# The router's last three pieces, its weights, rank products, list entries and scatters some slots later in the step

## The chip, the core and the metric

One Trainium2 chip, one core. The metric is the device time of one execution of the whole program in microseconds (us). TensorE is PE in the profile (PEld is its weight load), VectorE is DVE, ScalarE is ACT, GpSimd is POOL, SyncE is SP.

## What is computed

A vision-transformer layer on 16 images of 512 tokens with 256 features, plus one class token per image (513 rows). The parts of the reference that matter here:

```python
h = _L0_tok_ref(0, x, W0, W1, Wo)          # relu(x W0) * (x W1), then Wo; per token
h = concatenate([cls_tok, h], axis=1)
h = h + _L0_attn_ref(_layernorm(h), ...)   # quantised projections, 16 heads of 16
h = h + _L0_ffn_ref(_layernorm(h), ...)    # a router picks 2 of 8 experts for each token
# in _L0_ffn_ref:
router_probs = softmax(x_flat @ gate_w)
top_k_probs, top_k_idx = top_k(router_probs, 2)
top_k_probs = top_k_probs / sum(top_k_probs)
```

The kernel doesn't compute all experts for all tokens. It sorts the tokens by expert: for each token it finds the two best experts, the two weights, and a place in each of those experts' lists. Those list entries are written to memory by indirect DMAs (the scatters), and a second phase gathers the listed rows tile by tile.

## The kernel before

The program has a setup, a phase of steps that does everything up to the lists (some 1,680 us), and the expert phase. The change lies in the steps.

**Steps.** One step works on five images at once, each at another stage; in `body(T, P, C, W, X)` image T is in its token layer, P is normalised and projected, C has its attention scores computed, W finishes its attention, and X gets its second residual, its layer norm and its router. In step i, C is image i, T is i+2 and X is i-2. Steps -2 to 2 and 13 to 17 are written out; steps 3 to 12 are five laps of a hardware loop of two steps each, so that every engine jumps back after steps 4, 6, 8 and 10. Steps below are named by the image of C.

**Slots.** A step has 64 slots, `at` = 0 to 63 (group g = at // 16 of four heads, u = at % 16). In every slot PE multiplies one 128x512 block of scores (L493) and one of transposed scores (L502). DVE takes the row maxima of the first (`head_max`, L1147, a head maximum below) and ACT the exponential of the second (L823). PE has two banks for scores: its block of a slot waits for the head maximum of two slots before. In every fourth slot PE multiplies the exponentials by the values (`pv`, L511). Everything else is put into slots by hand: each engine's body asks `if X.ok and at == 47`. Each engine runs its own list in order, and semaphores join them.

**The router of X.** In slot 33 PE makes the logits. DVE's `router` has four pieces, in the slots of the table `ROUTER_AT`: piece 0 finds the largest logit, piece 1 (L1241 to L1243) its place and the one-hot `oh`, piece 2 (L1232 to L1239) masks it and finds the second one, piece 3 (L1241 to L1246) makes the second one-hot and `picked`, the sum of both. ACT makes one small exponential of the difference (L917), and DVE's `weights` (L1255 to L1257) the two weights. PE's `ranks` (L790 to L794) multiplies `picked` by a triangle of ones, which counts how many tokens before this one chose the same expert. DVE's `payload` (L1264 to L1272, then L1432) makes the places and the list entries. Then POOL issues the eight scatters of the image (L974), one for each slot in `SCATTER_AT`; the first waits for `payload`.

**What else is near it.** On DVE: L1436 (`pvd`, slot 36), L1298 (`hid`, 38), L1183 and L1184 (`den`, 39), L1193 and L1194 (`o_sb`, `pr`, 40), two statistics L1442 (slots 43, 44), L1461 and L1462 (45), L1447 and L1449 (46), L1155 and L1157 (end of 47), L1163 to L1456 (48), L1171 to L1472 (49), L1475 to L1478 (52), L1482 and L1484 (53). On PE: the transposes of the maxima (L647, slot 41) wait for `o_sb`; L725 (41, 42), `pv` (43, 47, 51), L750 (44), the token layer's output L562 (46, 49, 53, 57), L759 and L760 (51). On POOL: L1021 and L1025 (slot 35), L991 and L995 (41, after `pr`), L1029 (42, right behind them), which work on whole 128x1024 tiles; then nothing until the scatters; among these W's L1033 (slot 53, after the scatter of this slot), L991 and L995 again (57), and behind the last of them L1040 to L1048 (slot 60), which make the quantised `qi2` and `qic`. PE transposes these in slot 1 of the next step (L588), so L588 waits for L1048:

```python
if X.ok and at == 1:
    wait(pe, s("pool_qi2"), 2, X, 2)
```

Of the kernel before, what the change touches and what calls it, by code (L numbers as in the profile page):

```python
# [40 lines left out]
HIDDEN_AT = (14, 19, 22, 38)  # L41
OUT_AT = (46, 49, 53, 57)
STATS_AT = (53, 54, 60, 61)
ROUTER_AT = (34, 35, 37, 41)
SCATTER_AT = (52, 53, 54, 55, 56, 57, 58, 59)


C_ID, C_TRI = 0, 128
# [49 lines left out]
def fresh(eng, at, *batches):  # L98

    if batches[0].n is None or isinstance(batches[0].n, int):  # L100
        return batches
    n = batches[0].n
    copy = eng.alloc_register(f"lap_{batches[0].k}_{at}")
    eng.reg_mov(copy, n)
    n = eng.snap(copy, min_val=n.min_val, max_val=n.max_val)
    return [At(b.k, n, b.ok) for b in batches]


def wait(eng, sem, per, b, n):

    value = b.v * per + n
    if not isinstance(value, int) or value > 0:
        eng.wait_ge(sem, value)
# [31 lines left out]
def token_phase(nc, outer, images, x_t, cls, w0_t, w1_t, wo_t, attn_w_t, gate_w, consts, out,  # L145
# [12 lines left out]
    def s(name):  # L158

        if name not in sems:  # L160
            sems[name] = nc.alloc_semaphore(f"{name}_{stage}")
        return sems[name]
# [302 lines left out]
    def tensor_program(pe, stage):  # L465
# [49 lines left out]
        def body(T, P, C, W, X):  # L515
            for g in range(NG):
                for u in range(UNITS):
                    if u % 4 == 0:
                        T, P, C, W, X = fresh(pe, UNITS * g + u, T, P, C, W, X)
                        st, tg, mt = in_slot(g, P, C, W)  # L520
                    at = UNITS * g + u
# [193 lines left out]
                    if P.ok and at in (41, 42):  # L715
# [7 lines left out]
                        for t in (2 * k, 2 * k + 1):  # L723
# [1 line left out]
                                last = mm((d0, d1)[k][:, D * (t % 2):D * (t % 2 + 1)], xq[:, c, blk(t)],  # L725
                                          wq_int[:, 2, c, :], start=(c == 0), stop=(c == DC - 1))
                            last.then_inc(s("pe_v"), 1)
                    if X.ok and at == 47:
                        ranks(X, TB, 128, "", [("dve_oc", 1, W, 1)] if W.ok else [("dve_lg", 1, X, 1)])
                    if W.ok and at == 35:  # L730

# [52 lines left out]
        def ranks(b, nt, np_, x, free):  # L784

            wait(pe, s("dve_picked" + x), 1, b, 1)
            for name, per, at_, n in free:
                wait(pe, s(name), per, at_, n)
            a = picked[0:np_, :, :].rearrange("p t e -> p (t e)")
            mm(d2[0:np_, 0:nt * E], tri_bf[0:np_, 0:np_], a[:, 0:nt * E], start=True, stop=(nt == 1))  # L790
            for t in range(1, nt):
                mm(d2[0:np_, t * E:nt * E], ones_bf[0:np_, 0:np_], a[:, 0:(nt - t) * E], start=False, stop=(t == nt - 1))
            for t in range(nt):
                last = mm(d2[:, TB * E:(TB + 1) * E], ones_bf[0:np_, :], a[:, t * E:(t + 1) * E],  # L794
                          start=(t == 0), stop=(t == nt - 1))
            last.then_inc(s("pe_rk" + x), 1)

        if stage == STEPS:
            steps(pe, body)
# [11 lines left out]
    def scalar_program(act, stage):  # L811
# [13 lines left out]
        def body(T, P, C, W, X):  # L825
            for g in range(NG):
                for u in range(UNITS):
                    if u % 4 == 0:
                        T, P, C, W, X = fresh(act, UNITS * g + u, T, P, C, W, X)
                        st, tg, mt = in_slot(g, P, C, W)  # L830
                    at = UNITS * g + u
# [80 lines left out]
                    if P.ok and at == 40:  # L912
                        wait(act, s("pool_rk"), 1, P, 1)
                        f(parts["km"][:, :, :], rest[:, :, :], ACT.Copy).then_inc(s("act_km"), 1)
                    if X.ok and at == 39:
                        wait(act, s("dve_e"), 1, X, 1)
                        f(e21e[:, :], e21[:, :], ACT.Exp).then_inc(s("act_e"), 1)  # L917
                    if P.ok and at in (42, 43, 44, 45):
# [18 lines left out]
        if stage == STEPS:  # L937
            steps(act, body)
# [12 lines left out]
    def gpsimd_program(pool, stage):  # L951
# [16 lines left out]
        def scatter(b, nt, np_, x, pieces):  # L968

            if 0 in pieces:  # L970
                hold(pool, s("dve_pay" + x), 1, b, 1)
            for piece in pieces:
                k, t = divmod(piece, nt)
                g_.indirect_dma_start(out=list_dram, out_offset=bass.IndirectOffsetOnAxis(  # L974
                    ap=slot_i[0:np_, k, t:t + 1], axis=0), in_=pay[0:np_, k, t, :], in_offset=None) \
                    .then_inc(s("scattered"), 16)

        def body(T, P, C, W, X):
            for g in range(NG):
                for u in range(UNITS):  # L980
# [4 lines left out]
                    if u == 9 and tg[0].ok:  # L985
# [9 lines left out]
                        g_.tensor_tensor(o, o, cadd[:, :, :, :], ALU.add).then_inc(s("pool_add"), 1)  # L995
                    if X.ok and at in SCATTER_AT:
                        scatter(X, TB, 128, "", (SCATTER_AT.index(at),))
                    if P.ok and at == 0:
# [62 lines left out]
    def vector_program(dve, stage):  # L1061
        v = nc.vector

        class Link:
# [13 lines left out]
            def wait(self):  # L1078
                wait(dve, self.sem, self.per, self.b, self.n)
# [7 lines left out]
        def signal(ins, name, per, b, n):  # L1087

            ins.then_inc(s(name), 1)
            wait(dve, s(name), per, b, n)  # L1090
# [159 lines left out]
        def weights(b, x, nt, np_):  # L1250

            P = slice(0, np_)
            ch = Link("dve_chain_u" + x, 3, b)
            wait(dve, s("act_e" + x), 1, b, 1)
            ch(v.tensor_scalar(wts[P, 0, 0:nt], e21e[P, 0:nt], 1.0, None, ALU.add))  # L1255
            ch(v.reciprocal(wts[P, 0, 0:nt], wts[P, 0, 0:nt]))
            ch(v.tensor_tensor(wts[P, 1, 0:nt], e21e[P, 0:nt], wts[P, 0, 0:nt], ALU.mult))  # L1257

        def payload(b, x, nt, np_, rows):

            P = slice(0, np_)
            ch = Link("dve_chain_s" + x, 3, b)
            wait(dve, s("pe_rk" + x), 1, b, 1)
            ch(v.tensor_tensor(pos[P, 0:nt, :], d2[P, 0:nt * E].rearrange("p (t e) -> p t e", e=E),  # L1264
                               bcast(run[P, :], 1, nt), ALU.add))
            signal(v.tensor_tensor(run[:, :], run[:, :], d2[:, TB * E:(TB + 1) * E], ALU.add), "dve_rk" + x, 1, b, 1)
            ch(v.tensor_tensor(oh[P, :, 0:nt, :], oh[P, :, 0:nt, :], bcast(pos[P, 0:nt, :], 1, 2), ALU.mult))
            ch(v.tensor_reduce(out=slot[P, :, 0:nt], in_=oh[P, :, 0:nt, :], axis=AX.X, op=ALU.add))
            wait(dve, s("scattered"), 16 * 2 * TB, b, 0)
            signal(v.tensor_copy(slot_i[P, :, 0:nt], slot[P, :, 0:nt]), "dve_sl" + x, 1, b, 1)  # L1270
            signal(v.tensor_copy(pay[P, :, 0:nt, 0], bcast(rows, 1, 2)), "dve_row" + x, 1, b, 1)
            v.tensor_copy(pay[P, :, 0:nt, 1].bitcast(F32), wts[P, :, 0:nt]).then_inc(s("dve_pay" + x), 1)  # L1272
            ch.end(3)

        def body(T, P, C, W, X):
            for g in range(NG):
                for u in range(UNITS):
                    if u % 4 == 0:
                        T, P, C, W, X = fresh(dve, UNITS * g + u, T, P, C, W, X)
                        st, tg, mt = in_slot(g, P, C, W)  # L1280
                    at = UNITS * g + u
# [131 lines left out]
                    if P.ok and at in (27, 28, 30, 32):  # L1413
# [3 lines left out]
                        if fc == 0:  # L1417
# [6 lines left out]
                                               aqb[:, :], ALU.mult, ALU.mult).then_inc(s(f"dve_f{a}"), 1)  # L1424
                    if X.ok and at in ROUTER_AT:
                        router(X, "", TB, 128, pieces=(ROUTER_AT.index(at),))
                    if X.ok and at == 42:
                        weights(X, "", TB, 128)
                    if X.ok and at == 50:
                        payload(X, "", TB, 128, row[:, :])  # L1430
                        wait(dve, s("dve_pay"), 1, X, 1)
                        signal(v.tensor_scalar(row[:, :], row[:, :], float(SEQ), None, ALU.add), "dve_rows", 1, X, 1)  # L1432
# [71 lines left out]
        if stage == STEPS:  # L1504
            steps(dve, body)
# [352 lines left out]
```

## Time and profile before

| what | value |
|---|---|
| time, median of 3 runs | 2418.78 us (2418.55 to 2422.41) |
| span of the profiled execution | 2410.7 us, 8.1 below the median; no other time is given for this execution |
| PE busy | 2081.0 us (86%) |
| DVE busy | 1571.5 us (65%) |
| ACT busy | 1210.0 us (50%) |
| POOL busy | 911.2 us (38%) |
| mean granted clock of PE | 0.955 of full |

"Busy" is time in which the engine has an instruction under way. In the forty slices of the page, DVE stands at 7 to 9 tenths through most of the steps and at 3 in the expert phase; PE at 8 or 9 in both. The page's chain that ended last lies in the expert phase (PE L1743, L1728), which the change doesn't touch, so what follows is read from the timelines of the steps.

### The profile page before, as it was taken

How to read it: one execution, taken by the hardware profiler on the slowest of the kernel's cores; microseconds unless marked ns; L12 is line 12 of the kernel's file. 1: busy time of each engine (PE TensorE's matmuls, PEld its weight loads, DVE VectorE, ACT ScalarE, POOL GpSimd, SP SyncE). 2: the span in 40 equal slices, each digit the busy share in tenths (PEclk: the TensorE clock that was granted, in tenths of full speed). 3: DMA queues.
4: the chain of work that ended last, by engine and by line, in shares of the span. 5: the costliest groups of instructions: out<-in, count | busy, mean ns of one | idle time of the engine just before them, and what ended most of it. 6: DMA issues, size and time to landing. Idle time of an engine off the chain costs nothing. (4 is left out here: it accounts for less than half of the span.)

```text
span 2410.7 us, 46759 instructions
## 1 busy us (share of the span) xinstructions
PE 2081.0 (86%) x11964; PEld 1058.4 (44%) x12049; DVE 1571.5 (65%) x4036; ACT 1210.0 (50%) x2360; POOL 911.2 (38%) x894
## 2 busy tenths in 40 slices
PE   4889999999898898998998988861099999999997
PEld 2433444444343444443444433321066666666665
DVE  3477888887887887887888898841633333333332
ACT  1256566566565565665656666640444444444443
POOL 2222242332423423333234244133245555555554
PEclk9899999999999999999999998985599999999999
DMA  2322332322222323223232232201523333333332
GB/s 99 83 74 53 86 87 69 93 71 81 85 71 68 87 69 88 77 70 87 69 78 82 65 85 74 64 27 45 191 45 57 53 56 54 53 56 52 55 54 37
DMA packets 181071, 171.97 MB, mean 71 GB/s; under 512 B 40002, under 2 KB 169620, under 8 KB 180884
## 3 DMA queue, kind: packets, MB, share of 16 engines
q1 hardware_dynamic: 150612, 134.94, 20.1%
q0 software_dynamic: 30272, 34.80, 9.1%
q8 instruction: 86, 1.41, 0.3%
q14 instruction: 101, 0.83, 0.2%
HBM read 100.82 MB, written 68.93 MB: 70 GB/s over the span
## 5 line engine op out<-in xcount | busy, mean ns | idle before, releaser
L1147 DVE TENSOR_REDUCE mxs<-bank 128x1 f32<-128x512 f32 x1024 | 697.1, 685 | 205.0 <-PE bank L493 186.5
L823 ACT ACTIVATE pt<-bank 128x512 f32<-128x512 f32 x1024 | 588.5, 593 | 388.8 <-PE bank L502 369.3
L493 PE MATMUL bank<-ks,qs 96*128 96x512 bf16 x1024 | 397.9, 390 | 84.1 <-DVE mxs L1147 53.3
L502 PE MATMUL bank<-qs,ks 99*128 99x512 bf16 x1024 | 393.4, 385 | 9.2 <-ACT pt L823 8.7
L1697 POOL DMA_INDIRECT out<-y_sb,ids x136 | 214.6, 1578 | 273.3 <-DMA out<-y_sb,ids 193.7
L511 PE MATMUL bank<-pt,v_sb 128*32 128x512 f32 x2048 | 278.0, 615 | 0.0
L493 PEld LDWEIGHTS bank<-ks,qs 96*128 96x128 bf16 x1024 | 103.1, 101 | 357.5 <-DVE mxs L1147 214.0
L1826 DVE TENSOR_TENSOR hl<-bank,hh 128x512 bf16<-128x512 f32 x136 | 94.1, 692 | 210.7 <-ACT hh L1796 210.7
L1822 DVE TENSOR_TENSOR hid_e<-bank,act_g 128x512 f32<-128x512 f32 x136 | 94.1, 692 | 210.5 <-PE bank L1743 209.0
L974 POOL DMA_INDIRECT list_dram<-pay,slot_i x130 | 138.3, 1064 | 240.9 <-DVE pay L1272 206.7
L1743 PE MATMUL bank<-gu_l,xh 128*128 x544 | 206.9, 380 | 22.9 <-issue 21.2
L1743 PE MATMUL bank<-gu_h,xl 128*128 x543 | 206.6, 380 | 0.0
L991 POOL TENSOR_TENSOR cadd<-vcls,pr 128x256 f32<-128x256 f32 x64 | 41.1, 642 | 400.3 <-DVE pr L1194 400.0
L1743 PE MATMUL bank<-gu_h,xh 128*128 x477 | 181.9, 381 | 2.0 <-issue 1.2
L1688 POOL DMA_INDIRECT xg<-x_dram,ids x136 | 135.8, 998 | 64.7 <-issue 36.9
L1728 PE MATMUL bank<-dn_h,hh 128*128 x544 | 148.4, 273 | 3.0 <-DVE hl L1826 1.6
L1728 PE MATMUL bank<-dn_h,hl 128*128 x544 | 148.3, 273 | 0.0
L1728 PE MATMUL bank<-dn_l,hh 128*128 x544 | 148.3, 273 | 0.0
L502 PEld LDWEIGHTS bank<-qs,ks 99*128 99x128 bf16 x1024 | 100.2, 98 | 98.8 <-issue 38.6
L1789 ACT ACTIVATE act_g<-bank 128x512 f32<-128x512 f32 x136 | 81.2, 597 | 122.8 <-PE bank L1743 121.9
L542 PE MATMUL bank<-xt,w 128*128 128x512 f32 x256 | 130.8, 635 | 7.7 <-DMA xt<-x_t 7.7
L1784 ACT ACTIVATE y_sb<-bank,ids 128x256 f32<-128x256 f32 x136 | 64.3, 473 | 141.5 <-PE bank L1728 121.7
(283 smaller groups left out, 3529.2 us busy)
## 6 DMA issues: line engine op xcount, KB each, us to landing
qs<-qk_dram SPq DMA_DIRECT2D x128, 128.0 KB, 2.6
ks<-qk_dram SPq DMA_DIRECT2D x64, 192.0 KB, 3.4
xt<-x_t SPq DMA_DIRECT2D x16, 512.0 KB, 4.2
h_dram<-h_sb SPq DMA_DIRECT2D x16, 512.0 KB
qs<-qk_dram SPq DMA_DIRECT2D x128, 64.0 KB, 2.2
ks<-qk_dram SPq DMA_DIRECT2D x64, 128.0 KB, 3.4
hw<-h_dram SPq DMA_DIRECT2D x16, 512.0 KB, 4.3
out<-hw SPq DMA_DIRECT2D x16, 512.0 KB, 2.9
```

The source lines that it names most:

```text
L493: mm(score[u % 2][:, :], qs[0:QK, h, blk(t)], ks[0:QK, h, :], start=True, stop=True) \
L502: mm(scoret[u % 2][:, :], ks[0:QK + MROWS, h, blk(t)], qs[0:QK + MROWS, h, :], start=True, stop=True).then_inc(s("pe_st"), 1)
L511: last = mm(pv_bank[VW * j:VW * (j + 1), :], v_sb[:, b.par, t, g * GH + j, :], pt[:, t % 2, j, :], start=(t == 0), stop=(t == TB - 1))
L542: last = mm(d0[:, :], w0[:, c, blk(e)], xt[:, T.par, c, :], start=(c == 0), stop=(c == DC - 1))
L823: f(pt[:, t % 2, j, :], scoret[u % 2][:, :], ACT.Exp).then_inc(s("act_exp"), 1)
L974: g_.indirect_dma_start(out=list_dram, out_offset=bass.IndirectOffsetOnAxis(ap=slot_i[0:np_, k, t:t + 1], axis=0), in_=pay[0:np_, k, t, :] ...
L1147: v.reduce_max(mxs[:, t, g * GH + j:g * GH + j + 1], score[u % 2][:, :], AX.X).then_inc(s("dve_mx"), 1)
L1688: nc.gpsimd.indirect_dma_start(out=xg[:, i.place(ROWS), :], out_offset=None, in_=x2_dram, in_offset=rows(i)) \
L1697: nc.gpsimd.indirect_dma_start(out=out, out_offset=rows(i), in_=y_sb[:, i.place(2), :], in_offset=None, bounds_check=tokens - 1, oob_is_er ...
L1728: last = mm(y_b[:, 0:D], a[:, i.place(2), c, :], w[:, bass.ds(e, 1), c, :], start=(n == 1), stop=(n == 3 * FC))
L1743: last = mm(bank[k][:, :], a[:, k, c, :], w[:, bass.ds(e, 1), c, lo:lo + F], start=(m == 1), stop=(m == 3 * DC))
L1822: v.tensor_tensor(hid[:, :], up_b[i.place(2)][:, :], act_g[:, :], ALU.mult).then_inc(dve_hid, 1)
```

## The change

It moves work to other slots; no instruction is added or taken away. Piece 1 goes from slot 35 to 44, piece 2 from 37 to 45, piece 3 from 41 to 47, ACT's exponential from 39 to 46, the weights from 42 to 49, PE's ranks from 47 to 49, the payload from 50 to 51, and each scatter one slot on.

```diff
-ROUTER_AT = (34, 35, 37, 41)
-SCATTER_AT = (52, 53, 54, 55, 56, 57, 58, 59)
+ROUTER_AT = (34, 44, 45, 47)
+SCATTER_AT = (53, 54, 55, 56, 57, 58, 59, 60)
...
-                    if X.ok and at == 47:
+                    if X.ok and at == 49:
                         ranks(X, TB, 128, "", [("dve_oc", 1, W, 1)] if W.ok else [("dve_lg", 1, X, 1)])
...
-                    if X.ok and at == 39:
+                    if X.ok and at == 46:
                         wait(act, s("dve_e"), 1, X, 1)
...
-                    if X.ok and at == 42:
+                    if X.ok and at == 49:
                         weights(X, "", TB, 128)
-                    if X.ok and at == 50:
+                    if X.ok and at == 51:
                         payload(X, "", TB, 128, row[:, :])
```

DVE, from slot 43 to slot 45 of a written-out step, in the program with the change (L1147 is a head maximum, L1442 and L1461 the statistics of W, L1241 to L1243 and L1232 to L1239 the router's pieces 1 and 2):

```order
L1147 TENSOR_REDUCE mxs<-bank 128x1
L1241 SCALAR_TENSOR_TENSOR rtmp<-rtmp,cst 128x32
L1242 TENSOR_REDUCE ix<-rtmp 128x4
L1243 TENSOR_TENSOR oh<-cst,ix 128x32
L1442 BN_STATS bn<-o_sb 128x6
L1147 TENSOR_REDUCE mxs<-bank 128x1
L1232 SCALAR_TENSOR_TENSOR lg<-oh,lg 128x32
```

Before the change the two L1442 and the head maxima stood there alone; pieces 1 and 2 stood in slots 35 and 37.

POOL, from slot 42 to 60. Before:

```order
L1029 TENSOR_TENSOR part_kl<-rest,part_km 128x1024
L974 DMA list_dram<-pay,slot_i 75648x2 x2
L1033 TENSOR_SCALAR o_sb<-o_sb,nms 128x1024
L957 TENSOR_TENSOR rs<-msq,neg_half 128x1
L974 DMA list_dram<-pay,slot_i 75648x2 x3
L991 TENSOR_TENSOR cadd<-vcls,pr 128x256
L995 TENSOR_TENSOR o_sb<-o_sb,cadd 128x4x64
L974 DMA list_dram<-pay,slot_i 75648x2 x3
L1040 TENSOR_SCALAR o_sb<-o_sb,comb 128x256 x4
```

With the change:

```order
L1029 TENSOR_TENSOR part_kl<-rest,part_km 128x1024
L974 DMA list_dram<-pay,slot_i 75648x2
L1033 TENSOR_SCALAR o_sb<-o_sb,nms 128x1024
L957 TENSOR_TENSOR rs<-msq,neg_half 128x1
L974 DMA list_dram<-pay,slot_i 75648x2 x3
L991 TENSOR_TENSOR cadd<-vcls,pr 128x256
L995 TENSOR_TENSOR o_sb<-o_sb,cadd 128x4x64
L974 DMA list_dram<-pay,slot_i 75648x2 x4
L1040 TENSOR_SCALAR o_sb<-o_sb,comb 128x256 x4
```

All eight scatters still stand ahead of L1040; one instead of two stands ahead of L1033.

## Rows read from the trace of the kernel before

**Rows 1.** Who waited for whom, whole program: us in total, times, longest.

```profile
PE bank L493 <- DVE mxs L1147: 53.3, 91, 1.6
PE bank L588 <- POOL qic L1048: 26.3, 11, 17.2
```

**Rows 2.** Groups of instructions on DVE, shapes apart: count | busy us, mean ns | idle before.

```profile
L1243 DVE TENSOR_TENSOR oh<-cst,ix 128x32 f32<-128x32 f32 x32 | 34.9, 1092 | 1.1
L1246 DVE TENSOR_TENSOR picked<-oh 128x32 bf16<-128x32 f32 x16 | 19.9, 1241 | 0.6
```

**Rows 3.** Timeline of DVE, step 7: start us, us, line, operation, [idle before].

```profile
804.12 0.18 DVE L1232 SCALAR_TENSOR_TENSOR lg<-oh,lg 128x32 f32<-128x32 f32 x1
...
804.94 0.69 DVE L1147 TENSOR_REDUCE mxs<-bank 128x1 f32<-128x512 f32 x1
...
807.11 0.67 DVE L1147 TENSOR_REDUCE mxs<-bank 128x1 f32<-128x512 f32 x1
...
810.31 2.06 DVE L1246 TENSOR_TENSOR picked<-oh 128x32 bf16<-128x32 f32 x1
...
813.57 0.69 DVE L1147 TENSOR_REDUCE mxs<-bank 128x1 f32<-128x512 f32 x1
...
814.78 0.67 DVE L1147 TENSOR_REDUCE mxs<-bank 128x1 f32<-128x512 f32 x1
...
819.84 0.69 DVE L1147 TENSOR_REDUCE mxs<-bank 128x1 f32<-128x512 f32 x1 [0.36 <-PE bank L493]
...
824.84 0.17 DVE L1272 COPY pay<-wts 128x8 f32<-128x8 f32 x1
...
828.03 1.41 DVE L1482 TENSOR_SCALAR oc<-oc,ms 4x64 f32<-4x64 f32 x1
```

**Rows 4.** Timeline of POOL, the same step, to its end.

```profile
810.18 2.13 POOL L1029 TENSOR_TENSOR part_kl<-rest,part_km 128x1024 bf16<-128x1024 f32 x1
825.87 1.08 POOL L974 DMA_INDIRECT list_dram<-pay,slot_i  x1 [13.55 <-DVE pay L1272]
...
828.26 1.12 POOL L1033 TENSOR_SCALAR o_sb<-o_sb,nms 128x1024 f32<-128x1024 f32 x1
...
842.41 0.23 POOL L1048 TENSOR_SCALAR qic<-oc 4x64 bf16<-4x64 f32 x1
```

**Rows 5.** Timeline of PE, slots 40 to 44 of that step, and L588 after it.

```profile
805.93 0.39 PE L493 MATMUL bank<-ks,qs 96*128 96x512 bf16 x1
...
808.17 0.39 PE L647 MATMUL bank<-id_bf,nmp 128*12 128x128 bf16 x4 [0.68 <-DVE o_sb L1193]
...
809.82 0.38 PE L493 MATMUL bank<-ks,qs 96*128 96x512 bf16 x1
...
813.02 0.39 PE L493 MATMUL bank<-ks,qs 96*128 96x512 bf16 x1 [1.61 <-DVE mxs L1147]
...
842.77 0.62 PE L588 MATMUL bank<-id_bf,qi 128*128 128x128 bf16 x8 [0.80 <-POOL qic L1048]
```

**Rows 6.** Timeline of step 6, before which the loop doesn't jump; all engines.

```profile
706.50 0.39 PE L493 MATMUL bank<-ks,qs 96*128 96x512 bf16 x1
...
711.16 1.82 DVE L1257 TENSOR_TENSOR wts<-e21e,wts 128x4 f32<-128x4 f32 x1
...
724.36 0.17 DVE L1272 COPY pay<-wts 128x8 f32<-128x8 f32 x1
```

**Rows 7.** Timeline of PE behind the jump after step 6.

```profile
745.23 0.61 PE L493 MATMUL bank<-ks,qs 96*128 96x512 bf16 x1 [3.85 <-issue]
...
747.55 1.06 PE L588 MATMUL bank<-id_bf,qi 128*128 128x128 bf16 x8
```

**Rows 8.** Timelines of DVE and PE in step 16, which has no image in C.

```profile
1622.08 0.17 DVE L1272 COPY pay<-wts 128x8 f32<-128x8 f32 x1
...
1641.30 1.03 PE L588 MATMUL bank<-id_bf,qi 128*128 128x128 bf16 x8 [17.16 <-POOL qic L1048]
```

**Rows 9.** Busy time in a stretch: PE, PEld, DVE, ACT, POOL, PEclk, DMA share, GB/s.

```profile
739.00:743.00 4.00, 2.38 (x10) 0.20 (x8) 1.80 (x9) 0.60 (x1) 3.71 (x7) 0.50 0.25 23
```

## The prediction

> **What bounds the kernel now.** The page puts the end of the program into the expert phase, so a step can only help by ending sooner. I read the table of waits for PE first, because PE is the busiest engine of the steps. PE waits for DVE's head maxima 53.3 us in all, and for POOL's `qic` 26.3 us in 11 places, 17.2 of them in one place [rows 1]. So two other engines can end a PE wait: DVE inside a step, POOL at its end.
>
> Then the groups of DVE. L1243 handles 32 numbers in each partition and takes 1,092 ns on average; L1246 takes 1,241 ns [rows 2]. Operations of this size take about 0.2 us elsewhere. The timelines tell why: in step 7 L1246 starts at 810.31 and takes 2.06 us [rows 3], while POOL's L1029 runs from 810.18 for 2.13 us [rows 4]. DVE's operation ends when POOL's does. I call this a meeting. The 19.9 us of L1246 [rows 2] are 9 times 2.05 and 7 times 0.19, so 9 of the 16 images have this meeting. In the others the next operation with two inputs, L1257, meets L1029 instead and takes 1.82 us [rows 6], one slot later.
>
> Its price on PE: in step 7 the scores of slot 44 wait 1.61 us for a head maximum; the transposes of slot 41 wait 0.68 us for `o_sb`, which stands behind piece 2 [rows 5].
>
> At the end of the step POOL is the bound. The payload ends at 825.01 [rows 3], POOL's first scatter starts 0.86 us later, `qic` ends at 842.64 [rows 4], 17.6 us after the payload, and L588 starts at 842.77 after a wait of 0.80 us [rows 5]. So L588 follows the payload's end, and whatever PE gains before it is lost again. It is different where the loop jumps: PE stands idle 3.85 us, and L588 starts at 747.55 with no wait of its own [rows 7]; there what PE gains is kept.
>
> **The change, part by part.** All times are those of step 7 unless said.
>
> *Pieces 1 to 3 leave slots 35 to 41.* Piece 1's meetings in slot 35 lie beside 3 us of PE's products for the class token, and nothing waits; taking them away is worth nothing. Piece 2 took 0.82 us, 804.12 to 804.94 [rows 3]. Without it the head maximum of slot 40 starts at 806.33, which is PE's 805.93 [rows 5] plus 0.4 for the matmul, instead of 807.11 [rows 3]: 0.78 us sooner, and `o_sb`, L647 and POOL's L1029 with it. PE's slot 44, at 811.41 without its wait of 1.61, then comes to 810.6. DVE starts the head maximum of slot 44 at 811.0.
>
> *They come back in slots 44 to 49.* L1029 now ends at about 811.5 and piece 1 starts at 811.6, so the meeting is just missed. From there DVE never waits until the payload ends. Before, from the head maximum of slot 43 (813.57) to the payload's end (825.01) were 11.44 us. Of these 1.21 are slot 43's own (813.57 to 814.78, one head maximum and one L1442 at 0.6 each) and 0.36 a wait [rows 3], which leaves 9.87. To them come the 14 moved operations at 0.205 each (piece 2: four in 0.82), 2.87 us, and one more head maximum, since the payload moves behind that of slot 51, 0.6 us. That is 13.34 us, and the payload ends at 811.0 + 13.34 = 824.4 instead of 825.0: 0.6 us sooner. ACT's exponential moves too; ACT may hold its exponential of slot 46 for it by some 1.3 us, and PE needs that only in slot 48. PE's ranks (0.2 us) now stand behind the output of slot 49, and DVE has `picked` ready 1.5 us before.
>
> *Where no meeting with L1246 was* (step 6), the payload ended 724.53 - 706.50 = 18.0 us after slot 40 began [rows 6]; now it is 824.4 - 805.9 = 18.4, 0.4 us later.
>
> *The scatters.* All eight still precede `qic`, so the 17.6 us stay. L1033 moves ahead of one scatter: two took 2.39 us (825.87 to 828.26) [rows 4], one 1.2. DVE's L1482 meets L1033 (1.41 us) [rows 3], and the head maximum of slot 54 stands behind it. So PE's slot 56 and what follows come 0.6 + 1.2 = 1.8 us sooner in a step with the meeting and 1.2 - 0.4 = 0.8 sooner in one without.
>
> *The sum.* Seven steps (2, 5, 7, 9, 11, 12, 13) have the meeting and end at L588: 7 x -0.6 = -4.2. Step 3 has neither meeting nor jump: +0.4. Steps 4, 6, 8 and 10 end in a jump, the first with the meeting: -1.8 - 3 x 0.8 = -4.2. Steps 14 to 16 lack T and then P and C; DVE there had idle time in slots 35 to 37 that pieces 1 and 2 filled for nothing. In step 16 PE waits 17.16 us for POOL, whose chain starts behind the payload that ended at 1622.25 [rows 8]. The payload gets later by between 7 operations (1.5) and 14 (2.9); I take 2.3, since POOL's L995 still holds up what stands in front. Step 15: one head maximum and piece 1, +1.3. Step 14, the same with a meeting taken away: +0.4. Together: -4.2 + 0.4 - 4.2 + 4.0 = **-4.0 us**, against the profiled execution with its span of 2410.7. The median lies 8.1 us over that span, and I carry this over: 2418.8 - 4.0 = 2414.8. Bounds: nothing gained in any step and the last three at 2.9 each, +8.7; everything PE gains kept (8 x -1.8, 4 x -0.8, the last three at nothing), -17.6. I stay at the sum, because [rows 5] and [rows 8] show the wait for POOL in just these steps.
>
> **A rule that speaks against it.** The page SBUF — State Buffer of the Trainium skill (Who interferes with whom) says that GpSimd and a VectorE instruction with two SBUF inputs share a port, that the one that starts first holds it for its whole length, and that the other is blocked fully. The trace agrees: L1246 starts 0.13 us after L1029 and ends with it. By that rule L1029 starting 2 us later than I think would cost nearly its whole length again. That case is rival C, worked out from rows below.
>
> **The rivals.**
>
> A. *The gain stays.* If PE didn't hang on POOL at the end of a step, the port's 1.8 us would show in every step: the bound of -17.6, plus 4.0 in the last steps, -13.6, or 2405.2. Against it stands L588's wait [rows 5]. A smaller version, POOL's chain 0.5 us shorter in each step, gives another -4. 0.19 for both.
>
> B. *TensorE's clock* (the other side). PE gets further ahead, and POOL doesn't, so the wait at L588 grows from 0.8 to 0.8 + 1.8 - 0.6 = 2.0 us in seven steps. The granted clock was 0.50 from 739 to 743 [rows 9], at the jump, and the score matmul behind an idle time of 3.85 us took 0.61 us [rows 7] where it takes 0.39 at the full clock, so the engine was at 1.2 instead of 2.4 GHz. Behind 1.61 us of idle it still took 0.39 [rows 5]. If the wait of 2.0 us tips it, each such step pays some 2 us (the nine or so big matmuls of the slots right behind L588, 0.61 - 0.39 = 0.22 more for each): 7 x 2 = +14, or 2429. It decides the sign from three such steps on. [...] 0.12.
>
> C. *The meeting only moves.* Piece 1 starts 0.1 us after L1029 should end. If L1029 starts 1 us later than I think, or slot 44 comes sooner, DVE stops for what is left of it and the payload comes 0.4 us later than before instead of 0.6 sooner: 8 x +0.4 at L588, nothing kept at the jumps, +4.0 at the end, +7, or 2426. 0.09.
>
> D. *It doesn't do what it says for the time*: every gain is covered, the last steps' loss is small. 2418.8. 0.10.
>
> **How the numbers follow.** The forecast has 0.50. A measurement of this kernel can tell 0.2%, 4.8 us, from no change. The sum lies just inside that, so of the 0.50 I give 0.17 to faster and 0.33 to the same. A gives 0.17 to faster and 0.02 to the same. B and C give 0.15 to slower and 0.06 to the same; D's 0.10 are the same. Faster 0.34, same 0.51, slower 0.15. The range leaves out the far ends of A and B: 2406 to 2424.
>
> **What would show it.** Of the changed kernel: L1241, L1243 and L1246 at about 0.2 us on average; no wait of 1.6 us at slot 44; DVE without idle time from slot 44 to the payload; the payload's end 18.4 us after slot 40 in all steps alike; L588 waiting about 2 us for `qic` in the steps that don't jump; steps with the old meeting shorter by 0.6 us and step 16 longer by 2.3. The prediction is wrong if L588 no longer waits, if `qic` no longer ends 17.6 us behind the payload, or if the granted clock falls at L588.

## The result and the profile after

| kernel | median | ratio to the kernel before, 95% interval |
|---|---|---|
| before, 6 runs beside the change | 2418.66 us | 1 |
| the change, 6 runs | 2427.22 us | 1.0033 [1.0019, 1.0047] |
| the change again, 12 runs | 2424.73 us (before: 2414.77) | 1.0040 [1.0026, 1.0054] |

The change makes the kernel 8 to 10 us slower. The forecast was 4 us faster, and the measured time lies above its range. The profiled execution of the change took 2429.65 us over a span of 2427.8, so 1.8 us lie between span and time. Of the 8.1 us that the prediction carried over from the kernel before, then, most was that this one execution was faster than the median. This doesn't touch the difference, but the two profiled spans differ by 17.1 us and the medians by 8.6, so I compare steps and places and not the spans.

The waits of PE in the profile of the change, to set against [rows 1] (us in total, times, longest):

```profile
PE bank L493 <- DVE mxs L1147: 63.6, 102, 1.6
...
PE bank L588 <- POOL qic L1048: 26.8, 10, 14.0
```

PE waits 10.3 us more for head maxima, although the old meetings are gone. The groups of DVE (count | busy us, mean ns | idle before), against [rows 2]:

```profile
L1478 DVE SCALAR_TENSOR_TENSOR msq<-ms,msq 128x1 f32<-128x1 f32 x16 | 24.4, 1523 | 0.6
L1243 DVE TENSOR_TENSOR oh<-cst,ix 128x32 f32<-128x32 f32 x32 | 6.1, 192 | 1.1
L1482 DVE TENSOR_SCALAR oc<-oc,ms 4x64 f32<-4x64 f32 x16 | 4.3, 270 | 0.0
L1246 DVE TENSOR_TENSOR picked<-oh 128x32 bf16<-128x32 f32 x16 | 3.1, 192 | 2.0 <-DVE oh L1243 1.7
```

L1243 and L1246 are at 0.19 us, as forecast. But L1478, one number in each partition, now takes 1.52 us on average. Its group and its row in step 7 of the kernel before:

```profile
L1478 DVE SCALAR_TENSOR_TENSOR msq<-ms,msq 128x1 f32<-128x1 f32 x16 | 4.1, 256 | 0.6
```

```profile
826.99 0.16 DVE L1478 SCALAR_TENSOR_TENSOR msq<-ms,msq 128x1 f32<-128x1 f32 x1
```

The timeline of DVE in the change, step 7:

```profile
819.82 0.18 DVE L1241 SCALAR_TENSOR_TENSOR rtmp<-rtmp,cst 128x32 f32<-128x32 f32 x1
...
832.54 0.17 DVE L1272 COPY pay<-wts 128x8 f32<-128x8 f32 x1
...
833.95 0.16 DVE L1477 TENSOR_TENSOR msq<-ms 128x1 f32<-128x1 f32 x1
834.14 1.70 DVE L1478 SCALAR_TENSOR_TENSOR msq<-ms,msq 128x1 f32<-128x1 f32 x1
835.76 0.68 DVE L1147 TENSOR_REDUCE mxs<-bank 128x1 f32<-128x512 f32 x1
...
836.70 0.30 DVE L1482 TENSOR_SCALAR oc<-oc,ms 4x64 f32<-4x64 f32 x1
```

POOL in the same step, against [rows 4]:

```profile
817.63 2.14 POOL L1029 TENSOR_TENSOR part_kl<-rest,part_km 128x1024 bf16<-128x1024 f32 x1
833.57 1.08 POOL L974 DMA_INDIRECT list_dram<-pay,slot_i  x1 [13.80 <-DVE pay L1272]
834.71 1.11 POOL L1033 TENSOR_SCALAR o_sb<-o_sb,nms 128x1024 f32<-128x1024 f32 x1
836.02 0.56 POOL L957 TENSOR_TENSOR rs<-msq,neg_half 128x1 f32<-128x1 f32 x1 [0.20 <-DVE msq L1478]
...
840.67 0.63 POOL L991 TENSOR_TENSOR cadd<-vcls,pr 128x256 f32<-128x256 f32 x1 [0.30 <-issue]
...
850.59 0.23 POOL L1048 TENSOR_SCALAR qic<-oc 4x64 bf16<-4x64 f32 x1
```

L1478 ends at 835.84, L1033 at 835.82: a new meeting. L957 waits 0.20 us for L1478's result, L991 starts 0.30 us after the end of the scatter before it, where it was 0.02 in the kernel before, and `qic` ends 18.1 us behind the payload (832.71 to 850.82), not 17.6. And PE, slot 55 and then L588 at the start of the next step, against [rows 5]. Here and below the L588 "of" a step is the one that follows it:

```profile
836.50 0.39 PE L493 MATMUL bank<-ks,qs 96*128 96x512 bf16 x1 [1.61 <-DVE mxs L1147]
...
850.96 0.62 PE L588 MATMUL bank<-id_bf,qi 128*128 128x128 bf16 x8 [1.13 <-POOL qic L1048]
...
851.62 0.61 PE L493 MATMUL bank<-ks,qs 96*128 96x512 bf16 x1
852.02 0.63 PE L502 MATMUL bank<-qs,ks 99*128 99x512 bf16 x1
```

The wait of 1.61 us that stood at slot 44 stands at slot 55 now, the same 1.61. Behind L588 the matmuls of 512 columns take 0.61 to 0.63 us instead of 0.39: PE is at 1.2 GHz. The stretch behind L588, by its windows (PE, PEld, DVE, ACT, POOL, PEclk, DMA share, GB/s), in the change and then in the kernel before:

```profile
850.90:854.90 4.00, 3.94 (x21) 1.36 (x22) 2.98 (x12) 2.69 (x8) 0.94 (x1) 0.59 0.70 184
```

```profile
842.70:846.70 4.00, 3.93 (x39) 1.78 (x40) 3.00 (x12) 2.67 (x8) 0.96 (x1) 1.00 0.92 246
```

PE is busy throughout in both, but gets through 21 matmuls in the change and 39 before. From L588 to the scores of slot 6 are 6.89 us in step 7, before the change 5.30. Between 264 and 1520 us the trace shows 15 stretches at a granted clock of 0.5 in the change (12 in its second profile, e13 below), 6 in the kernel before.

Two theories remained. **M**: the meeting of L1478 with L1033 is the loss. **K**: the clock is. Against them **P** (the later payload by itself costs) and **N** (the clock follows lost time and costs nothing).

### The profile page after: what moved, and what is told of

It is laid out like the page before. It is cut to its first block and busy times, and to the rows that moved or that the text cites. A ratio compares the mean times of both kernels' runs of the same rounds, so it can differ in the third digit from the quotient of the medians.

```text
span 2427.8 us, 46770 instructions
## 1 busy us (share of the span) xinstructions
PE 2099.7 (86%) x11964; PEld 1064.1 (44%) x12049; DVE 1521.7 (63%) x4036; ACT 1213.8 (50%) x2360; POOL 910.8 (38%) x894
## 5 line engine op out<-in xcount | busy, mean ns | idle before, releaser
L1147 DVE TENSOR_REDUCE mxs<-bank 128x1 f32<-128x512 f32 x1024 | 696.3, 685 | 267.7 <-PE bank L493 257.7
L493 PE MATMUL bank<-ks,qs 96*128 96x512 bf16 x1024 | 403.3, 395 | 83.2 <-DVE mxs L1147 63.6
L502 PE MATMUL bank<-qs,ks 99*128 99x512 bf16 x1024 | 399.3, 391 | 6.9 <-ACT pt L823 6.4
L511 PE MATMUL bank<-pt,v_sb 128*32 128x512 f32 x2048 | 285.5, 631 | 0.0
L493 PEld LDWEIGHTS bank<-ks,qs 96*128 96x128 bf16 x1024 | 104.2, 102 | 371.1 <-DVE mxs L1147 230.5
L991 POOL TENSOR_TENSOR cadd<-vcls,pr 128x256 f32<-128x256 f32 x64 | 40.5, 633 | 403.2 <-DVE pr L1194 401.3
```

The lines of the kernel that those rows point to most:

```text
L493: mm(score[u % 2][:, :], qs[0:QK, h, blk(t)], ks[0:QK, h, :], start=True, stop=True) \
L502: mm(scoret[u % 2][:, :], ks[0:QK + MROWS, h, blk(t)], qs[0:QK + MROWS, h, :], start=True, stop=True).then_inc(s("pe_st"), 1)
L511: last = mm(pv_bank[VW * j:VW * (j + 1), :], v_sb[:, b.par, t, g * GH + j, :], pt[:, t % 2, j, :], start=(t == 0), stop=(t == TB - 1))
L1147: v.reduce_max(mxs[:, t, g * GH + j:g * GH + j + 1], score[u % 2][:, :], AX.X).then_inc(s("dve_mx"), 1)
```

## The experiments

All ratios are to the kernel before on the same chip; its median there was 2414.8 to 2416.7 us, 2 to 4 below that of the result's table, so a range in microseconds is best read as a difference. In e5, e10 and e12 added lines shift the numbers: L493 is L494 there, L588 is L592 (their L588 is the added work), L1048 is L1052.

### e1_scatters_back

```diff
-SCATTER_AT = (53, 54, 55, 56, 57, 58, 59, 60)
+SCATTER_AT = (52, 53, 54, 55, 56, 57, 58, 59)
```

> The changed kernel with the scatters back in slots 52 to 59, so that two of them stand ahead of L1033 again; the payload stays in slot 51. Theory M (in the changed kernel DVE's L1478, which has two inputs in SBUF, meets POOL's L1033: 1.70 us in step 7; the head maxima of slots 53 and 54 and PE's slot 55 wait behind it, and POOL's chain behind L1033 gets 0.5 us longer): L1478 back at 0.16 us, L1482 at about 1.4 instead, qic 17.6 us behind the payload instead of 18.1, and the time back at that of before or a little below, 2413 to 2419 us. Theory P (it is the later payload and list entries that cost; the meeting is covered): L1478 at 0.16 as well, but the time stays within 2 us of the changed kernel's, 2425 to 2429.

Measured: 2415.91 us, ratio 1.0007 [0.9996, 1.0017]. L1478 is at 0.16, `qic` 17.6 us behind the payload. M's time came, P's didn't. One expectation failed: L1482 mostly misses L1033 too (0.23 us), so this kernel has no meeting from slot 44 to 57 in most steps. It is the kernel that the prediction described: counted from slot 40, PE's slot 57 comes 1.9 to 2.2 us sooner than before in a step with the old meeting and 0.8 to 1.1 in one without (forecast 1.8 and 0.8), and the wait at L588 is 2.29 us (forecast 2.0):

```profile
843.65 1.00 PE L588 MATMUL bank<-id_bf,qi 128*128 128x128 bf16 x8 [2.29 <-POOL qic L1048]
...
844.72 0.61 PE L493 MATMUL bank<-ks,qs 96*128 96x512 bf16 x1
```

It still isn't faster. Little of PE's lead is kept at L588, since slot 40 to `qic` takes 36.2 us in step 7, before 36.7; and behind L588 the clock falls in most steps (6.8 to 6.9 us to slot 6 in steps 3, 5, 7, 11 and 12, 13 stretches at 0.5).

### e2_router_alone

```diff
-SCATTER_AT = (53, 54, 55, 56, 57, 58, 59, 60)
+SCATTER_AT = (52, 53, 54, 55, 56, 57, 58, 59)
-                    if X.ok and at == 51:
+                    if X.ok and at == 50:
                         payload(X, "", TB, 128, row[:, :])
```

> Only the router's move: pieces 1 to 3, ACT's exponential, the weights and the rank products as in the change; the payload back in slot 50 and the scatters back in 52 to 59. The payload then stands in front of one more head maximum, so if DVE does not wait for PE's rank products (which end 0.5 us before the scores of slot 49 in the changed kernel) the payload ends 18.0 us after slot 40 instead of 18.6, and qic 0.6 us sooner. Theory Q (everything at L588 follows the payload): 0.6 us in each of the eight steps without a jump below e1_scatters_back, ratio about 0.998, 2409 to 2413. If DVE waits for the rank products, as e1_scatters_back: 1.000 to 1.001.

Measured: 2416.86 us, ratio 1.0012 [0.9999, 1.0025]. The time is about that of the second case, but DVE doesn't wait for the rank products, so the reason is neither case's. The payload does end 0.6 us sooner (18.0), but the head maxima of slots 51 and 52 stand behind it, and PE waits for them; the clock falls there, and the token layer's output L562 takes 3.03 us, where it takes 1.89 in slot 57:

```profile
827.08 0.61 PE L493 MATMUL bank<-ks,qs 96*128 96x512 bf16 x1 [1.56 <-DVE mxs L1147]
```

With the payload in slot 51 and the same scatters, e1 is no slower than this (1.0007), so the payload's move to slot 51 is not what costs.

### e3_scatters_alone

```diff
 (the kernel before)
-SCATTER_AT = (52, 53, 54, 55, 56, 57, 58, 59)
+SCATTER_AT = (53, 54, 55, 56, 57, 58, 59, 60)
```

> The kernel before with the scatters alone moved a slot on (53 to 60); pieces, weights, ranks and payload as before. Theory M: POOL's L1033 now starts about 1.2 us sooner, at the time at which L1478 starts (826.99 in step 7 of the kernel before), so L1478 takes 1 us or more, PE waits over 1 us for a head maximum at slot 55, qic 0.3 to 0.5 us later behind the payload, and the time goes up by 5 to 12 us: 2424 to 2431. Theory P: one scatter fewer ahead of L1033 changes nothing by itself, 2417 to 2421; the loss came with the router's move.

Measured: 2421.94 us, ratio 1.0029 [1.0019, 1.0040]. The scatters alone bring most of the loss. Here DVE's L1478 and, in the second fence, POOL's L1033 and L957:

```profile
829.05 1.15 DVE L1478 SCALAR_TENSOR_TENSOR msq<-ms,msq 128x1 f32<-128x1 f32 x1
```

```profile
829.07 1.11 POOL L1033 TENSOR_SCALAR o_sb<-o_sb,nms 128x1024 f32<-128x1024 f32 x1
830.38 0.56 POOL L957 TENSOR_TENSOR rs<-msq,neg_half 128x1 f32<-128x1 f32 x1 [0.20 <-DVE msq L1478]
...
835.03 0.63 POOL L991 TENSOR_TENSOR cadd<-vcls,pr 128x256 f32<-128x256 f32 x1 [0.29 <-issue]
```

Two parts of the expectation failed. The time lies between the ranges of both theories, though as a difference, +7.0 us, it is inside M's 5 to 12. And PE doesn't wait at slot 55 for over 1 us; its slots 50 to 57 are 0.1 us shorter than before. What is left is POOL's chain: in steps 3 to 12 `qic` is 18.1 to 18.3 us behind the payload, 0.5 to 0.7 more. The trace has as many stretches at 0.5 as the kernel before (6), and by step 16 its L588 is 4.6 us behind that of the kernel before (1645.91 against 1641.30). But this was the fastest of eight executions, 7.4 us below their median, with the highest mean granted clock of them, 0.958; the median of the eight is 0.9555, of the kernel before beside them 0.958. So the trace prices the meeting on POOL's chain at some 4 to 5 us; the clock may have a part in the rest of the 7.0. This is still the clearest run on the term "the 17.6 us stay".

### e4_one_input

```diff
-v.scalar_tensor_tensor(msq2[:, 1:2], ms2[:, 1:2], EPS, msq2[:, 0:1], ALU.add, ALU.subtract)
+v.scalar_tensor_tensor(msq2[:, 1:2], d0[:, 1:2], EPS, msq2[:, 0:1], ALU.add, ALU.subtract)
```

> The changed kernel; only L1478 reads its first input from the PSUM bank d0 instead of its copy ms2 in SBUF, so it has one SBUF input (msq2) instead of two. Same values, same slots, same number of operations. Theory M: L1478 at about 0.2 us though L1033 starts where it did; PE's wait at slot 55 falls from 1.6 to under 0.7 us; L1482 may be held by L1033 for up to 1.4 us as before the change; the time 2412 to 2419. Theory P: L1478 gets short, but the time stays at 2425 to 2429.

Measured: 2416.60 us, ratio 1.0006 [0.9995, 1.0017]: one operand read from PSUM takes away 6.5 to 8 us of the 8 to 10. The clock doesn't rise by it: the median of the mean granted clocks is 0.949, as in the change (0.949 and 0.950). So the meeting costs by itself. (The trace of e4, with 11 stretches at 0.5, is of its fastest execution.) L1478 starts 0.57 us ahead of L1033, as in the change, and takes 0.16:

```profile
826.76 0.16 DVE L1478 SCALAR_TENSOR_TENSOR msq<-bank,msq 128x1 f32<-128x1 f32 x1
...
827.80 0.68 DVE L1482 TENSOR_SCALAR oc<-oc,ms 4x64 f32<-4x64 f32 x1
```

L1482, now the one that overlaps L1033 (827.33 to 828.44), is held to its end. PE waits 0.1 us at slot 55 and 0.26 at slot 56, `qic` is back at 17.6, and L588 now waits 2.30 us. The page SBUF — State Buffer of the Trainium skill (Who interferes with whom) says that a VectorE instruction with at most one SBUF input, outside the two-port performance modes, doesn't contend with GpSimd; this pair of kernels agrees, 0.16 against 1.70 us for L1478 with nothing else changed.

### e5_filled and e10_filled_less

PE computes for nothing ahead of the wait for `qic`. e5 has FILL = 6, e10 has 3:

```diff
-                        wait(pe, s("pool_qi2"), 2, X, 2)
...
                             wait(pe, s("act_v"), TB, C, TB)
+                        if P.ok:
+                            for _ in range(FILL):
+                                mm(d0[:, :], id_bf[:, :], wq_int[:, 0:2, 0, :], start=True, stop=True)
+                        wait(pe, s("pool_qi2"), 2, X, 2)
```

> The changed kernel with six more matmuls of 512 columns (outputs thrown away, into d0) on PE in slot 1 ahead of its wait for qic: PE computes there instead of standing idle; it adds work and takes no wait away. Theory K (a good part of the 8.6 us is TensorE's clock, which in the changed kernel falls to 0.5 behind the wait at L588 in steps where it didn't fall before; from L588 to slot 6 is 6.89 us in step 7 against 5.30 before): from L588 to slot 6 about 5.3 us again in steps 3, 5, 7, 9, 11, mean clock up by 0.005 or more, and the time down by 4 to 10 us to 2417 to 2423, though 1.3 to 2.3 us of matmuls per step are added where PE waited 1 to 2 us. Theory N (the clock follows the lost time, but costs nothing, since DVE and POOL set the pace): time within 2 us of the changed kernel's or up to 8 us above it, 2425 to 2435.

> The changed kernel with three instead of six matmuls of 512 columns (outputs thrown away) ahead of PE's wait for qic; they take 3 x 0.22 = 0.7 us at the full clock, less than the wait of 1.13, so they add nothing to the path. In e5_filled six of them kept L588 to slot 6 at 5.3 us (6.9 in the changed kernel), but lay on the path themselves at 1.3 to 2.8 us, and the time stayed (ratio 1.0036 against 1.0033). Theory K (the fallen clock costs by itself): L588 to slot 6 at 5.3 us in steps 3, 5, 7, 9, 11 and time 4 to 10 us below the changed kernel: 2414 to 2421. Theory N (the clock costs nothing, the pace is set by POOL and DVE): 2422 to 2427.

Measured: e5 2425.28 us, ratio 1.0036 [1.0022, 1.0050]; e10 2419.39 us, 1.0008 [0.9997, 1.0018]. By its time alone e5 is N's case, above K's range. With six, L588 to slot 6 was back at 5.3 us in all steps without a jump up to step 13, but where the clock was low behind a jump the six took 2.76 us (749.23, start of step 7), more than the 1.6 us that they were to save. With three (0.81 us), the start of step 8 of e10, behind step 7 and without a jump, reads:

```profile
844.71 0.81 PE L588 MATMUL bank<-wq_int,id_bf 128*128 128x512 bf16 x3
845.93 0.62 PE L592 MATMUL bank<-id_bf,qi 128*128 128x128 bf16 x8 [0.41 <-POOL qic L1052]
...
846.60 0.39 PE L494 MATMUL bank<-ks,qs 96*128 96x512 bf16 x1
```

The matmul behind L588 is at 0.39 again, the stretches at 0.5 fall from 15 to 7, the median of the granted clocks rises from 0.949 and 0.950 to 0.9545, and the time falls by 6 to 8 us although work was added. So K holds against N: the clock is a loss of its own, and e5 alone would have misled. The meeting was still in e10 in full (mean 1.53 us).

### e12_one_input_filled

Both edits together: e4's operand and e10's three matmuls.

> e4_one_input (no meeting of L1478 with L1033, ratio 1.0006) together with the three filling matmuls of e10_filled_less: the change without either of its two new losses. If the two are what turned the forecast gain into a loss, then L588 to slot 6 takes 5.3 us, the steps without a jump are about 0.5 us shorter than in the kernel before, and the ratio is 0.998 to 0.999 (the forecast of this change was 0.9983). If it stays at 1.000 or above, the sum of the prediction had a third mistake.

Measured: 2411.49 us, ratio 0.9984 [0.9972, 0.9996]. Without its two losses the change is worth about what was forecast, 0.9983. The agreement in the last digit is luck, as the interval says, and the clock isn't held everywhere: L588 waits 1.58 us still, and in steps 3, 5 and 11 the way to slot 6 takes 6.9. One control wasn't run: the three matmuls in the kernel before. What they might give there would have to come off the gain that e12 shows for the change.

### e13_change_again

No edit.

> The changed kernel unchanged, beside the others on the same chip: ratio to the kernel before 1.0020 to 1.0045, and L1478 at 1.5 us on average again; L588 to slot 6 over 6.5 us in most steps without a jump.

Measured: 1.0040 [1.0026, 1.0054], L1478 at 1.52 us as in the first profile. L588 to slot 6 was over 6.5 us in four of the nine steps without a jump, so not in most: 3, 7, 9 and 14. In the first profile it was in 3, 5, 7, 11 and 14; which of the steps lose the clock changes from execution to execution.

### e7, e8, e9 and e11: the last two scatters behind qic

The gain at L588 is given back because `qic` follows eight scatters. L1040 needs only DVE's `comb`, so two scatters can stand behind L1048. In e7 and e8 the table is (52 to 57, 61, 62), on e1 and on the kernel before; in e9 and e11 it is (53 to 58, 61, 62), on e4 and on the change:

```diff
-SCATTER_AT = (53, 54, 55, 56, 57, 58, 59, 60)
+SCATTER_AT = (53, 54, 55, 56, 57, 58, 61, 62)
```

> As e1_scatters_back (router's pieces moved as in the change, scatters from slot 52), but the last two scatters in slots 61 and 62, behind L1040 to L1048 on POOL, which only need DVE's comb (ready at 836.79 in step 7 of e1, L1040 started at 839.86). Theory Q (the change does shorten PE's slots, and the gain is given back at L588, since qic follows the payload by eight scatters): L1040 about 2.5 us sooner, qic 15.1 us behind the payload, PE's wait of 2.29 us at L588 gone, the clock at full there (slot L588 to slot 6 in 5.3 us), so 2 to 3.5 us in each of the eight steps without a jump: 2390 to 2403 against 2415.7 for the kernel before. Theory R (DVE, saturated since slot 44, is the bound; PE gets held for head maxima in the next step instead): L588's wait goes, but the time stays at 2408 to 2417.

> The kernel before with only the last two scatters moved to slots 61 and 62, behind L1048. Theory Q: L1040 can start 1.7 us sooner (838.99 to DVE's comb at 837.25, step 7), L588's wait of 0.80 goes and no more, 0.8 us in each of eight steps and 1.7 in the last ones, 2402 to 2411; the difference between this kernel and e7_two_behind (6 us or more) is what the router's move is worth once it isn't given back. Theory R: both the same within 3 us.

> The changed kernel with both repairs: L1478 reads its first input from PSUM (e4_one_input) and the last two scatters stand in slots 61 and 62 behind L1048 (scatters otherwise as in the change, from slot 53). Theory Q: as e7_two_behind, 2388 to 2403. Theory R: 2408 to 2417.

> The change with only its last two scatters in slots 61 and 62, behind L1048; L1478 keeps its two SBUF inputs and its meeting with L1033. Theory M+Q (the meeting costs PE 1.2 us or more at slot 55, and without the wait at L588 nothing gives that back): clearly slower than e9_one_input_two_behind (ratio 0.988), by 5 to 14 us, ratio 0.990 to 0.994. If the meeting only mattered through the clock at L588: within 2 us of e9, 0.987 to 0.989.

| kernel | router's pieces moved | meeting of L1478 | median | ratio |
|---|---|---|---|---|
| e8 | no | no | 2407.87 us | 0.9968 [0.9956, 0.9979] |
| e11 | yes | yes | 2405.12 us | 0.9959 [0.9944, 0.9974] |
| e7 | yes | no | 2394.74 us | 0.9910 [0.9896, 0.9924] |
| e9 | yes, one input | no | 2388.69 us | 0.9880 [0.9863, 0.9896] |

Theory Q holds for the times, and in e7 and e9 `qic` comes 15.1 us behind the payload. The same move of the router's pieces that is worth nothing while L588 waits (e1, 1.0007) is worth 14 us once it doesn't (e8 to e7). e11's loss against e9, 19 us, is above the 5 to 14 that I expected: with PE no longer waiting at L588, the meeting costs the most. (The two medians are from different chips, so the 19 us are the difference of the ratios.) e9 is the fastest of all, 1.2% below the kernel before, and leaves out nothing of the computation. Its L588 follows the matmul before it without a wait. One part of Q failed: from L588 to slot 6 are 6.9 us in e7 and e9 too, not 5.3. It isn't the clock, since the matmuls of 512 columns take 0.39 there. It is the next wait, which L957 (`rstd`), now behind the two scatters, passes on through `qbd`:

```profile
835.27 0.61 PE L588 MATMUL bank<-id_bf,qi 128*128 128x128 bf16 x8
...
835.94 0.39 PE L493 MATMUL bank<-ks,qs 96*128 96x512 bf16 x1
...
839.42 0.42 PE L598 MATMUL bank<-fq,kbd 128*32 128x256 f32 x2 [0.98 <-DVE qbd L1323]
```

## Why the prediction was wrong

- **The old meetings**: right. L1243 and L1246 at 0.19 us, no wait at slot 44. Slot 44 was to start 4.7 us after slot 40 and starts 4.68 after it (814.11 to 818.79); piece 1 was to miss L1029's end by 0.1 us and misses it by 0.05 (819.77 to 819.82), so rival C's first half didn't come. C's 2426 is near the measured time all the same, by another way: a meeting moved, but to L1478.
- **The payload 18.4 us after slot 40 in all steps**: nearly. It is 18.6 in one step of a lap and 18.9 in the other. In step 7 DVE waits 0.26 us behind piece 2, where it was to have no idle time.
- **"All eight still precede `qic`, so the 17.6 us stay"**: this step failed. They became 18.1 to 19.0 in steps 3 to 12. In step 7 they are 18.1, and with the 0.2 us of the payload that eats the whole gain: slot 40 to `qic` takes 36.7 us before and after (-0.5 and +0.5). In step 3, which had no old meeting, it is +1.0 us instead of +0.4, and in steps 6, 8 and 10 +1.4 to +1.9. e3 shows this term with the scatters' move alone, +7.0 us, of which its trace has 4.6.
- **"L1033 moves ahead of one scatter ... DVE's L1482 meets L1033"**: this is the omission behind it. I moved POOL's operation past one scatter and asked only about the DVE operation that it had met before. L1478 started 1.98 us behind the payload's end in the kernel before (825.01 to 826.99); with one head maximum less in between it starts 1.4 behind it, and L1033, which had started 3.2 behind it, now starts 2.0 behind it. PE's slot 57, which was to be 1.8 us sooner after slot 40, was 0.6 sooner in step 7, and later by 0.4 to 1.8 in steps where no old meeting paid for it. The rule quoted in the prediction, that the one that starts first holds the port, would have let L1478 pass. The sentence of the Trainium skill behind it (SBUF — State Buffer, Who interferes with whom) says "Whoever issues first", not who starts first, and no view here shows when an operation is issued. Rows of before already spoke against using the start times so closely: L1482 started 0.23 us ahead of L1033 and was held to its end [rows 3, 4].
- **Rival B, the clock, held at 0.12**: it came, beside the meeting. Its form was right (PE ahead, POOL not, 1.2 GHz behind L588), with 1.6 us for a step where 2 was estimated. It needed no wait of 2.0 us: 1.13 was enough in many steps. Runs e10 and e12 price it at 5 to 8 us, where the rival said 14.
- **The last three steps**: +4.0 forecast, and from L588 of step 13 to L588 of step 16 the two traces differ by 4.1 us, but that is luck: the shares are 0, +3.4 and +0.7 us where +0.4, +1.3 and +2.3 were forecast. In step 15 the clock was low behind L588 of step 14 (6.82 us to slot 6 against 5.30); in step 16 the payload came 2.1 us later, as forecast, but `qic` only 17.6 us behind it, where it had been 19.0.
- **The sum**: -4.0 with neither, e12 measures -3.9 (0.9984 of 2415). With the meeting (+6 to +8, e4 and e10 to e12) and the clock (+5 to +8) it comes to about +9; measured +8 and +10. That the meeting costs without a change of clock is shown by e4, which has the change's clock, and that the clock costs with the meeting in place by e10.

Two of the three signs that the prediction named for being wrong came: `qic` no longer ended 17.6 us behind the payload, and the granted clock fell at L588.

Why L991 lags its scatter can be read off the traces. It needs DVE's `pr` (L1194). In step 7 of the kernel before, `pr` ended 0.08 us before the scatter ahead of L991 started (832.67 and 832.75):

```profile
832.50 0.17 DVE L1194 TENSOR_TENSOR pr<-pcls,rinv 128x16 f32<-128x16 f32 x1
```

```profile
832.75 0.96 POOL L974 DMA_INDIRECT list_dram<-pay,slot_i  x1 [0.31 <-issue]
833.73 0.65 POOL L991 TENSOR_TENSOR cadd<-vcls,pr 128x256 f32<-128x256 f32 x1
```

In the change DVE, held up by the meeting, ends it 0.82 us after that start (840.23 and 839.41), still before the scatter's end at 840.37:

```profile
840.06 0.17 DVE L1194 TENSOR_TENSOR pr<-pcls,rinv 128x16 f32<-128x16 f32 x1
```

```profile
839.41 0.96 POOL L974 DMA_INDIRECT list_dram<-pay,slot_i  x1 [0.31 <-issue]
840.67 0.63 POOL L991 TENSOR_TENSOR cadd<-vcls,pr 128x256 f32<-128x256 f32 x1 [0.30 <-issue]
```

Over all 14 traces, L991 follows the scatter by at most 0.03 us in 116 of the 117 places where `pr` ended no later than 0.77 us after the scatter's start, and by 0.22 us or more in all 87 where it ended later. e2 has the same lag (0.46 us in step 7) with L1478 at 0.16, so what counts is DVE's delay and not L1478's meeting as such.

What stays open is which steps lose the clock, and why POOL loses 0.3 us even when `pr` is there before the scatter ends.

## What to carry to other kernels

When an operation of one engine is moved in time, list everything of the other engine within 1 us of its new start, not only what it met in the old place. Here the new meeting cost PE the same 1.61 us as the one removed, and POOL 0.5 us more, because DVE's held operations feed POOL. A gain inside a step is worth nothing while the step's end waits on another chain, and a longer wait there can cost clock as well: shorten that chain in the same edit. If a tiny VectorE operation can't be moved out of the way, see if one of its two inputs is still in PSUM.

## What the runs showed that I had not expected

- A DVE operation is held although it starts first by the profile. In step 7 of the change L1478 starts 0.57 us before L1033, during the scatter, and ends with L1033; in e3 0.02 us before; L1482 of the kernel before 0.23. In e1 L1482 starts at 828.35, 0.77 us ahead of L1033's 829.12, and takes 0.23. L1477, 0.76 us ahead in the change, takes 0.16. The longest lead that was still held is 0.74 us (L1478 in step 16 of the change, 1.87 us), the shortest at which L1478 with both inputs in SBUF passed is 0.73 (step 15 of e7, 0.16 us). The page Perfetto Trace Analysis of the Trainium skill (GPSIMD Engine Instruction) says to treat GpSimd's spans in a profile as unreliable; that fits, but no run here shows when L1033 really begins to read.
- The same wait at L588 can go either way. It is 1.13 us in steps 5, 7, 9 and 11 of e3, and the clock holds (L588 to slot 6 in 5.30 us); in its step 3, at 1.14, it falls (6.83). In steps 3, 5, 7 and 11 of the change it is 1.13 or 1.14 too, and the clock falls (6.8 to 6.9); in its step 9, again at 1.13, it holds. So the length of this wait alone doesn't decide it.
- Added work can make a kernel faster: three thrown-away matmuls in each step took 6 to 8 us off the change.
